# Earlier rows for the first batch, a shorter fill between indirect transfers, and eight filler transposes for forty-eight

## What is computed

```
def ffn(x):                                    # stage A, and again as stage C
    probs = softmax(x @ gate_w.T + gate_b)
    topk_vals, topk_idx = top_k(probs, 2)
    h = relu(einsum('bsd,edh->bseh', x, w1) + b1)
    expert_out = einsum('bseh,eho->bseo', h, w2) + b2
    return sum(take(expert_out, topk_idx) * topk_vals)

x = x + 0.5 * ffn(layernorm(x))                # stage A
x = x + attention(layernorm(x))                # stage B, low-rank keys and values
x = x + 0.5 * ffn(layernorm(x))                # stage C
```

## Time and profile before

| | us |
|---|---|
| median of three runs | 1193.15 |
| lowest, highest | 1191.34, 1196.9 |
| the profiled execution | 1193.1 |
| its span, first to last instruction | 1191.3 |
| busy in the span: PE, ACT, DVE, POOL | 1139.1, 912.3, 721.9, 714.4 |

### The profile page before, as it was taken

The page is one execution under the profiler, slowest core; times in us unless marked ns, Lnnn a source line. Parts: engine busy times, 40 slices in busy tenths (PEclk is TensorE's granted clock), DMA queues, the critical chain, the costliest instruction groups (busy, mean ns, idle before and its releaser), DMA issues.

```text
span 1191.3 us, 26036 instructions
## 1 busy us (share of the span) xinstructions
PE 1139.1 (96%) x8278; PEld 759.2 (64%) x8278; DVE 721.9 (61%) x2254; ACT 912.3 (77%) x2255; POOL 714.4 (60%) x868
## 2 busy tenths in 40 slices
PE   7999998999999999999999999999999999999996
PEld 5677575676675557576666666666665456757675
DVE  4785568566785657375663676566657545647335
ACT  2348678678897989796898888888888887888431
POOL 3146568584848888028887653886701875268655
PEclk8998998999999999999999999999999889999988
DMA  8075573756645176656565636566732156548872
GB/s 287 1 251 167 176 224 110 243 159 204 203 136 149 47 227 210 177 149 183 178 210 154 181 123 183 161 206 196 211 107 63 41 159 178 148 148 249 257 257 73
DMA packets 159883, 202.07 MB, mean 170 GB/s; under 512 B 16938, under 2 KB 103426, under 8 KB 159747
## 3 DMA queue, kind: packets, MB, share of 16 engines
q1 hardware_dynamic: 144196, 168.90, 46.2%
q0 software_dynamic: 15360, 31.49, 9.1%
q10 hardware_dynamic: 192, 0.02, 0.0%
HBM read 152.50 MB, written 47.84 MB: 168 GB/s over the span
## 4 chain that ended last, share of the span: by engine, by line
PE 69%; POOL 10%; ACT 10%; issue 5%; DVE 3%; DMA 2%; SPq 0%; POOLq 0%; ACTq 0%; DVEq 0%
PE psum L1587 63%; ACT probs L1193 4%; ACT psum L1202 3%; POOL Y L1111 3%; POOL pause L1075 3%; PE psum L1707 2%; POOL slots_C L1091 2%; POOL slots_A L1091 2%; PE psum L1615 1%; PE psum L1772 1%; DVE neg_m L1541 1%; ACT hg L1239 1%; PE psum L1674 1%; DMA results_C<-ys 1%; ACT xnB L1158 1%
## 5 line engine op out<-in xcount | busy, mean ns | idle before, releaser
L1541 DVE TENSOR_REDUCE neg_m<-psum 128x1 f32<-128x512 f32 x512 | 317.6, 685 | 155.1 <-PE psum L1587 155.0
L1587 PE MATMUL psum<-nat 32*128 32x512 f32 x2048 | 364.4, 643 | 2.5 <-DVE ys L1521 1.4
L1202 ACT ACTIVATE psum<-psum,neg_m 128x512 f32<-128x512 f32 x512 | 341.6, 682 | 27.7 <-DVE neg_m L1541 26.9
L1193 ACT ACTIVATE probs<-psum 128x512 f32<-128x512 f32 x512 | 266.6, 630 | 43.2 <-PE psum L1587 41.6
L1587 PEld LDWEIGHTS psum<-nat 32*128 32x128 f32 x2048 | 130.6, 185 | 94.7 <-issue 24.3
L1075 POOL MEMSET pause<- 128x900 f32 x212 | 183.5, 866 | 0.1
L1587 PEld LDWEIGHTS psum<-xg_T,wt 128*128 128x128 f32 x1296 | 157.5, 195 | 40.2 <-ACT probs L1193 12.5
L1587 PE MATMUL psum<-xg_T,wt 128*128 128x128 f32 x1296 | 171.8, 283 | 5.3 <-DMA wt<-packed 3.5
L1587 PEld LDWEIGHTS psum<-wt,hg 128*128 128x128 f32 x1296 | 156.3, 196 | 31.6 <-ACT psum L1202 11.5
L1091 POOL DMA_INDIRECT slots_A<-xnA,posA x120 | 118.0, 983 | 95.0 <-DMA xs<-slots_A 44.9
L1587 PE MATMUL psum<-wt,hg 128*128 128x128 f32 x1296 | 166.7, 283 | 8.4 <-ACT psum L1202 3.7
(11 more groups left out here) (192 smaller groups left out, 1424.5 us busy)
## 6 DMA issues: line engine op xcount, KB each, us to landing
wt<-packed SPq DMA_DIRECT2D x324, 320.0 KB, 4.1
xs<-slots_A SPq DMA_DIRECT2D x36, 256.0 KB, 4.6
results_A<-ys SPq DMA_DIRECT2D x36, 256.0 KB
xs<-slots_C SPq DMA_DIRECT2D x36, 256.0 KB, 5.3
results_C<-ys SPq DMA_DIRECT2D x36, 256.0 KB
X<-in_L_attn_x_dram SPq DMA_DIRECT2D x16, 256.0 KB, 8.3
out_dram<-X SPq DMA_DIRECT2D x16, 256.0 KB
packed<-probs SPq DMA_DIRECT2D x1, 2560.0 KB, 8.2
```

Source lines behind the costliest of these rows:

```text
L1193: act.activation(probs[:, kt, j, :], at.banks()[j][:], ACT.Exp).then_inc(a_done, 1)
L1202: act.activation(at.banks()[j][:], at.banks()[j][:], ACT.Exp, bias=neg_m[:, g, n, j:j + 1], accum_out=sums[:, g, n, j:j + 1]).then_inc(S[" ...
L1541: V_.tensor_reduce(neg_m[:, g, n, j:j + 1], at.banks()[j][:], AX.X, ALU.max, negate=True).then_inc(S["r_done"], 1)
L1587: return nc.tensor.matmul(dst, w, m, start=start, stop=stop)
```

## The change

Four edits. The rank tables move into a function that GpSimd calls after its rows of batch 0, so the rows come ahead of the 25 table instructions. The filler transposes ahead of the first `xTf` go from 12 rounds (48) to 2 rounds (8). The fill between two pairs of indirect transfers, one operation of 900 columns, becomes two of 150, each waited for by itself. ScalarE's first relus wait for `setup_dve` 2 in place of 3.

```diff
 A_SHIFT = [-175.05, -104.61, -123.83, -99.41, 64.11, 103.6, 44.98]
 C_SHIFT = [47.89, 123.22, 85.45, 65.66, 50.22, -503.25, 389.89]
 KEEP = {("B", 0, "xT", 0): 10, ("B", 2, "xT", 0): 2, ("B", 4, "mrow", 1): 2, ("B", 13, "mrow", 0): 1,
-        ("A", 0, "xTf", 0): 12, ("A", 6, "h", 0): 1, ("C", 8, "h", 4): 2, ("C", 11, "logits", 0): 1,
+        ("A", 0, "xTf", 0): 2, ("A", 6, "h", 0): 1, ("C", 8, "h", 4): 2, ("C", 11, "logits", 0): 1,
         ("C", 10, "y", 1): 2, ("C", 12, "xTf", 0): 1}
 GAP = 3.4

...
         gw_T, gate_bias = sb("gw_T", [P, EXPERTS]), sb("gate_bias", [P, EXPERTS])
         first_wins = sb("first_wins", [P, EXPERTS])
         ident = sb("ident", [P, P])
-        pause = sb("pause", [P, 900])
+        pause = sb("pause", [P, 2, 150])
         ones = sb("ones", [P, P])
         minus_one = sb("minus_one", [1, P])
         earlier = sb("earlier", [P, P])
...
                                pattern=[[1, P]], channel_multiplier=-1)
             pool.affine_select(out=up_to[:], in_=up_to[:], compare_op=ALU.is_ge, fill=0.0, base=0,
                                pattern=[[1, EXPERTS], [-1, EXPERTS]], channel_multiplier=0)
-            for t in range(T_MAX):
-                linked(pool.affine_select(out=same_expert[:], in_=same_expert[:], compare_op=ALU.not_equal, fill=1.0,
-                                          base=-t * EXPERTS, pattern=[[-1, EXPERTS]], channel_multiplier=1))
-            pool.tensor_copy(spread[:, 0:EXPERTS], same_expert[:])
-            for t in range(T_MAX):
-                last = pool.affine_select(out=spread[:, (t + 1) * EXPERTS:(t + 2) * EXPERTS], in_=same_expert[:],
-                                          compare_op=ALU.is_gt, fill=0.0, base=t * EXPERTS, pattern=[[0, EXPERTS]],
-                                          channel_multiplier=-1)
-            last.then_inc(consts_made, 1)
+
+            def rank_tables():
+
+                for t in range(T_MAX):
+                    linked(pool.affine_select(out=same_expert[:], in_=same_expert[:], compare_op=ALU.not_equal, fill=1.0,
+                                              base=-t * EXPERTS, pattern=[[-1, EXPERTS]], channel_multiplier=1))
+                pool.tensor_copy(spread[:, 0:EXPERTS], same_expert[:])
+                for t in range(T_MAX):
+                    last = pool.affine_select(out=spread[:, (t + 1) * EXPERTS:(t + 2) * EXPERTS], in_=same_expert[:],
+                                              compare_op=ALU.is_gt, fill=0.0, base=t * EXPERTS, pattern=[[0, EXPERTS]],
+                                              channel_multiplier=-1)
+                last.then_inc(consts_made, 1)

             def add(at):

...
             def apart(at):

                 if at.step in after_pair:
-                    linked(pool.memset(pause[:], 0.0))
+                    for n in range(2):
+                        linked(pool.memset(pause[:, n, :], 0.0))

             def scat(at):

...
                     last = pool.tensor_scalar(xn[s][:, xn_place(s, b) + n, :], X[:, b % X_RING, n, :], rstd[s][:, n:n + 1],
                                               shift[s][:, n:n + 1], ALU.mult, ALU.add)
                 last.then_inc(S["rows_done"], 1)
+                if (s, b) == ("A", 0):
+                    rank_tables()

             walk("POOL", {"scaled": scaled, "add": add, "scat": scat, "gat": gat})

...
                 if at.k >= DHG_RING:
                     act.wait_ge(d_full, at.count("d_full", "dy", (at.k - DHG_RING) // UNITS))
                 if at.stage == "A":
-                    act.wait_ge(setup_dve, 3)
+                    act.wait_ge(setup_dve, 2)
                     act.activation(hid[:, at.k % DHG_RING, :], at.banks()[0][:], ACT.Relu, bias=b1_T[:, at.k:at.k + 1]).then_inc(a_done, 1)
                 else:
                     act.activation(hid[:, at.k % DHG_RING, :], at.banks()[0][:], ACT.Relu).then_inc(a_done, 1)
```

## The result

The changed kernel took **1283.15 us** (median of four runs, 1275.32 to 1287.09), beside 1195.03 us for the kernel before (1191.34 to 1197.28). The ratio is 1.073, with a 95% interval of 1.067 to 1.080. I had forecast 1185.3 us in a range of 1178.0 to 1191.5, and had given 4 chances in 100 to anything slower by more than 0.5%. No rival of the prediction comes near this time; the worst of them ended at 1198.3.

A forecast was written before the change was run, and what follows sets the result against it. TensorE, busy 96% of the span, was taken as the bound, with waits for GpSimd. Start 2.4, end 2.4, middle 2.0 and VectorE's blocks 1.0 sum to 7.8 us: 1193.1 - 7.8 = 1185.3 us, range 1178.0 to 1191.5.

The forecast's parts named there:

- The start: rows, fillers, first dh: At the launch's start, rows would begin at 6.7 and the first dh at 10.2 in place of 14.65, 4.4 us earlier.
- The start's clock: TensorE would meet the first dh probably at 1.2 GHz, a loss of about 2.0 us, between nothing and 5.0.
- rival (c): Fillers don't raise TensorE's clock, so the start brings its whole 4.4 us: 1183.3 us; chance 0.03.
- What the lead is worth in the end: The start would bring 4.4 - 2.0 = 2.4 us, between -0.6 and 4.4, and keep it.
- rival (a): The low clock uses up the start's lead: start -0.6 to 0, the rest 4 to 5 us, 1189 us; chance 0.20.
- The length of the gap: From the end of one transfer to the next, with the short fill: 0.86 us in place of 1.14.
- What the gap saves: Each shortened fill on GpSimd would save 0.28 us, counted where the chain passes through it, in two places.
- The end and the middle: Shorter fills save 2.4 us before the last gathers and 2.0 of TensorE's 3.50 us stall at 193.63.
- Rival (b): The shorter stall near 190 us no longer brings the clock's fall, 3.9 us more won: 1181.4 us; chance 0.16.
- VectorE's blocks: VectorE instructions such as the cast at line 1560, held up by the fill, would gain 1.0 us, between 0 and 2.
- The prediction's own sign of being wrong as a whole: TensorE's half-rate time growing by over 10 us would show the whole forecast wrong.
- rival (d): Slower: the start's low clock carries on into later light stretches, with 20 us more of it 1198.3 us; chance 0.07.

The follow-up runs named there:

- e5_after_tile900: The changed kernel with the fill's tile kept at 900 columns, of which two operations write the first 300; 1179.45 us, 0.991 of before.
- r1_after_again: The changed kernel run once more without an edit, in a later set; 1291.70 us, 1.079 of before.
- b1_head_fill700: The changed kernel with one fill of 700 columns in place of two of 150; 1183.59 us, 0.993 of before.
- e2_head_fill900: The changed kernel with the old fill, one operation of 900 columns; 1189.84 us, 0.999 of before.
- r5: The kernel before with one fill of 700 columns; 1185.62 us, 0.993 of before.
- e1: The kernel before with two fills of 150 columns inside the old tile of 900, start as before; 1207.82 us, 1.012 of before.
- r2: The kernel before with two fills of 150 columns in the tile of 900, run in a later set; 1285.20 us, 1.074 of before.
- e6: The kernel before with the change's two fills of 150 columns and its tile cut to 300 columns; 1179.33 us, 0.992 of before.
- e3_fill_2x347: The kernel before with two linked fills of 347 columns, together as long as the old one; 1188.12 us, 0.996 of before.
- s1_spread_388: The kernel before with the fill split: 388 columns ahead of every pair and 388 between its two transfers; 1192.16 us, 1.000 of before.
- a1: The kernel before with one fill of 150 columns; 1555.29 us, 1.304 of before.

## Why the prediction was wrong, point by point

**The start: rows, fillers, first dh.** Right. The prediction had the rows at 6.7 and the first dh at 10.2; they came at 6.61 and 10.29. The batch norm of batch 1 is held by its load as said, at 17.95, and VectorE's first centring came at 25.07, forecast 25.3.

**The start's clock.** Right for the first trace, and not a constant. Six records of dh took 5.46 us, nearly twice the 2.81 of the earlier trace rows and thus at 1.2 GHz, inside the 4.5 to 5.6 that I had given. The granted clock reads 1.00 there, as it did for the slow fillers of before. But the same head gave 2.81 us, that is 2.4 GHz, in e5_after_tile900 and r1_after_again, and 5.09 in b1_head_fill700:

```profile
10.34 2.81 PE L1593 MATMUL psum<-xT_F,probs 128*128 128x512 f32 x6 [0.78 <-ACT xT_F L1262]
```

I had let the rise follow the start of continuous work at a fixed distance, from the one rise that the trace of before shows. It doesn't: before the first dh these launches have the same work, and the clock is up in one and not in the other. With 48 fillers it was up in all fourteen kernels that have them (2.81 us), with 8 in two of six, so rival (c), by which fillers do nothing for the clock, got no support.

**What the lead is worth in the end.** 2.4 us were predicted. e2_head_fill900, the head alone, gave 0.999 of before, -1.5 us with an interval from -5 to +2, and b1 and r5 are alike. So it is small, and whether it is there the runs can't tell; rival (a) is as good a reading. The sentence "I let 2.4 stand" had no support: the lead has to pass VectorE, where only 1.6 us could. In the trace of e2 ScalarE is 4.2 us ahead of before at 12 us and 1.5 at 30.

**The length of the gap.** Right. The fill was to give 0.86 us from transfer to transfer and gave 0.80 (0.53 for the two, 0.27 behind them), against 1.14.

**What the gap saves.** This is the step that failed: "0.28 us saved for each", with the fill taken as mere delay. I priced what GpSimd gains and asked which chain passes through it. I didn't ask what the other engines pay when transfers come 10% faster. They pay far more than GpSimd gains: the short fill alone cost 15 us in e1 and 90 in r2, where the prediction had it save 5.4 (2.4 at the end, 2.0 in the middle, 1.0 in the blocks). There were two signs: the constant GAP = 3.4 in the planner, printed in the diff, which holds pairs 3.4 us apart, and the period of 3.39 us that the fill makes of it. A fill of an unused tile has no use but to keep something apart, so its shortening needed a rival of its own, "the spacing was needed". With its worst end unknown, the range should have been open on the slow side, and the 4 chances in 100 for slower were far too few.

**The end and the middle.** Where nothing stalls, they came as worked out. In e5 the stall of 3.50 us before the rows has shrunk to 1.66 and ends with another event, and the end from the first gather to the last addition takes 37.9 us (1128.61 to 1166.54), predicted 38.3:

```profile
188.17 1.08 PE L1680 MATMUL psum<-ident,xnA 128*128 128x128 f32 x4 [1.66 <-ACT psum L1208]
...
1128.61 0.99 POOL L1115 DMA_INDIRECT Y<-results_C,posC  x1 [8.77 <-issue]
...
1166.54 2.30 DVE L1512 SCALAR_TENSOR_TENSOR X<-Y,gateC,X 128x128 f32<-128x128 f32 x8
```

Rival (b), that the shorter stall takes its clock with it, did not come in: the granted clock in e5 is 0.50 in 190 to 195 and 0.77 in 195 to 200, so it still falls. In the change itself the end brought nothing; from the first gather to the last addition it takes 41.1 us.

**VectorE's blocks.** The mechanism is there; its worth stays open. I took 1.0 us from one cast. Over all VectorE instructions that took over 0.1 us more than the shortest of their kind, that excess comes to 37 us before (46 in e2) and 9 in e3_fill_2x347, whose fill has the old spacing and a break in the middle. That kernel gained 4.5 us (0.996, interval 0.993 to 0.999). But in s1_spread_388 the excess is down to 15 us, and nothing is gained (1.000, 0.998 to 1.003). So the term may have been up to 4.5 us or near nothing. The rule of the Trainium skill that the prediction weighed (SBUF — State Buffer, section "Who interferes with whom"), that the second to come waits out the whole instruction of the first, agrees: with the break in the middle three quarters of the blocked time are gone.

**The sum.** Without the stalls, in e5 (the change with the tile at its old size), it is worth 0.9% on the second chip: 10 us (6 to 15) for 7.8 predicted. That the two are close is in part luck, since two errors cancel: e6, the short fill alone, gains the same (0.992) where the prediction had 5.4, and the start, at 2.4 in the sum, adds nothing that can be seen. Which term of the fill was too small the runs don't tell. On the machine of the result the prediction was wrong by 98 us. Of the 94 us that the profiled span grew, 47 are stretches without a matmul; the rest shows as busy time of TensorE, 49.5 us more of it. The granted clock, 0.954 over the span in place of 0.970, is a part of that: (1 - 0.954) x 1285.4 = 59 us of clock withheld against (1 - 0.970) x 1191.3 = 36, so at most 23 us. What makes up the remainder is not shown. The clock seems to fall with the stalls: it is 0.979 in e2 and 0.86 in a1. The prediction's own sign of being wrong as a whole, half-rate time up by over 10 us, thus came true (23 us withheld are 46 at half rate), but not by rival (d), which had it come from the start: e2 has the same start and loses nothing.

## What to carry to other kernels

An operation whose result nobody reads may be holding two things apart. Before you shorten it, ask for what, and give "it was needed" a price that is open upwards. When an indirect transfer is made to come sooner, look at all engines, not at GpSimd alone: waits in the bursts that end with "remote", an increment long after the instruction that made it, are the sign. And take such a measurement on more than one chip: the short fill made the old kernel 0.8% faster on one, and 1.2 and 7.4% slower on two others. A period of 3.22 us (fill of 700 columns) gained 0.7% on the one chip where it was tried, which stalls at 3.04; but 3.13 us already lost 0.6% on another chip, so its margin is small, and the fill of before is the safer choice.

## What the runs showed of the hardware that I had not expected

- Pairs of indirect transfers every 3.04 us (0.97 us for each issue) can hold up the hand-over from TensorE to ScalarE and VectorE for 2 to 5 us at a time: TensorE's semaphore increments come up to 7.2 us after the instruction that makes them, ScalarE's and VectorE's don't. At 2.77 us they come up to 15.4 us late, single waits reach 10 us on ScalarE, 13 on TensorE and 22 on VectorE, and the kernel takes 30% longer. Halving the bytes or the rows of the scatters doesn't help (1.299, 1.316).
- Even spacing and spacing by pairs are alike (1.000 at 3.38 us).
- Chips, or something else that changes from set to set, differ in it: the ratio of the short fill at 3.04 us was 0.992, 1.012 and 1.074, with the kernel before within 0.5% in all sets.
- TensorE's clock at the start of a launch can be up or down with the same work ahead: 2.81 or 5.46 us for the same six records after 8 fillers. After 48 fillers it was 2.81 in all fourteen kernels.
